# Delta rule: one key product a chunk, write keys through memory, exponents moved, output copies first

## The reference

```python
rk = rk / jnp.maximum(jnp.linalg.norm(rk, axis=-1, keepdims=True), 1e-12)      # read keys
wk = jnp.pad(rk[:, :, :-1], ((0, 0), (0, 0), (1, 0), (0, 0)))                   # write keys: one token later
L_mask = jnp.tril(jnp.exp(jnp.tril(cum[..., :, None] - cum[..., None, :])))     # decays inside a chunk
M = jnp.tril(-(wk_scaled @ jnp.swapaxes(wk, -1, -2)) * L_mask, -1)
A = solve_triangular(eye - M, eye, lower=True, unit_diagonal=True)
intra = jnp.tril(rk @ jnp.swapaxes(wk, -1, -2) * L_mask, -1)
# step over chunks, carrying the state S (128 x 128 for each batch and head)
v_new = A_i @ vsc_i - A_i @ wkd_i @ S
o_i = rkd_i @ S + intra_i @ v_new
S = ced_i * S + wkp_i @ v_new
```

## Time and profile before

| what | value |
|---|---|
| median of 3 runs | 2408.51 us (2408.32 to 2412.16) |
| time of the profiled execution | 2399.99 us |
| its span, first to last instruction | 2398.3 us |
| mean granted PE clock over the span | 0.965 |
| PE busy over the span | 2197.5 us (92%) |
| DVE, ACT, POOL busy | 1843.5, 1646.8, 1449.4 us |
| the first stage | 0 to 404.2 us, PE busy 336.67 us of it |

### The profile page before, as it was taken

The page is one execution under the profiler, slowest core; times in us unless marked ns, Lnnn a source line. Parts: engine busy times, 40 slices in busy tenths (PEclk is TensorE's granted clock), DMA queues, the critical chain, the costliest instruction groups (busy, mean ns, idle before and its releaser), DMA issues.

```text
span 2398.3 us, 36952 instructions
## 1 busy us (share of the span) xinstructions
PE 2197.5 (92%) x12464; PEld 1788.7 (75%) x12464; DVE 1843.5 (77%) x2832; ACT 1646.8 (69%) x2715; POOL 1449.4 (60%) x1026
## 2 busy tenths in 40 slices
PE   6799897999999999996999999999999999999986
PEld 4788796998898898884667667676676765776765
DVE  5574453667766666677989989989899899898995
ACT  6775542555555556666887788787877877888774
POOL 0236563111111113336988989889889898898895
PEclk8899998999999999997999999999999999999988
DMA  8434544566666654444655655555555555565563
GB/s 291 85 56 111 112 125 136 181 236 232 234 230 230 233 209 152 133 126 154 219 169 190 198 184 186 194 186 202 176 186 195 199 187 177 185 211 177 178 208 101
DMA packets 235434, 430.22 MB, mean 179 GB/s; under 512 B 35089, under 2 KB 117457, under 8 KB 235234
## 3 DMA queue, kind: packets, MB, share of 16 engines
q1 hardware_dynamic: 229090, 410.87, 53.0%
q0 software_dynamic: 6144, 16.79, 2.2%
HBM read 353.61 MB, written 73.96 MB: 178 GB/s over the span
## 4 chain that ended last, share of the span: by engine, by line
PE 54%; DVE 13%; issue 9%; ACT 9%; DMA 6%; POOL 6%; SPq 1%; another core or an unknown queue 1%; POOLq 1%; DVEq 0%; ACTq 0%
PE pb L1641 11%; PE pb L1614 11%; DVE pb L2094 6%; PE pb L2406 5%; PE pb L2411 5%; PE pb L994 3%; PE pb L2305 2%; PE pb L2432 2%; PE pb L2321 2%; DVE UU L2100 2%; DMA XB<-xnd 2%; PE pb L2330 2%; DMA CC<-bcd 2%; POOL UU L2019 2%; POOL UU L2027 1%
## 5 line engine op out<-in xcount | busy, mean ns | idle before, releaser
L2019 POOL TENSOR_TENSOR UU<-dx,BB 128x1024 f32<-128x1024 f32 x256 | 614.6, 2409 | 112.0 <-DMA BB<-bcd 83.6
L2231 ACT ACTIVATE pb<-dt,al 128x512 f32<-128x512 f32 x512 | 339.5, 685 | 149.4 <-DVE UU L2100 147.8
L2100 DVE TENSOR_TENSOR UU<-pb,CC 128x512 f32<-128x512 f32 x512 | 351.3, 686 | 24.3 <-DMA CC<-bcd 6.5
L2094 DVE TENSOR_TENSOR_SCAN pb<-pb,hs,UU 128x512 f32<-128x512 f32 x256 | 328.5, 1283 | 10.7 <-ACT pb L2231 7.4
L2094 DVE TENSOR_TENSOR_SCAN pb<-pb,UU 128x512 f32<-128x512 f32 x256 | 313.0, 1223 | 8.5 <-ACT pb L2231 7.9
L1381 POOL TENSOR_TENSOR clo_b<-craw_b,chi_b 128x1024 fp32r<-128x1024 f32 x22 | 62.3, 2830 | 405.9 <-ACT chi_b L1444 405.9
L1531 DVE TENSOR_TENSOR HL<-HF,HH 128x512 fp32r<-128x512 f32 x220 | 159.6, 728 | 179.9 <-ACT HH L1436 165.7
L2406 PE MATMUL pb<-HAh,WH 128*128 128x512 f32 x1024 | 282.7, 419 | 7.0 <-DVE dt L2075 5.1
L1431 ACT ACTIVATE HF<-pb,BU 128x512 f32<-128x512 f32 x192 | 132.3, 689 | 219.4 <-PE pb L1614 191.9
L2411 PE MATMUL pb<-HAl,WH 128*128 128x512 f32 x1024 | 259.7, 396 | 0.0
L1641 PE MATMUL pb<-W2h,HH 128*128 128x256 f32 x880 | 256.0, 291 | 1.0
(11 more groups left out here) (336 smaller groups left out, 4891.0 us busy)
## 6 DMA issues: line engine op xcount, KB each, us to landing
WH<-fhd SPq DMA_DIRECT2D x176, 512.0 KB, 3.5
BB<-bcd SPq DMA_DIRECT2D x256, 256.0 KB, 4.7
CC<-bcd SPq DMA_DIRECT2D x256, 256.0 KB, 5.0
raw<-in_w1a SPq DMA_DIRECT2D x23, 1024.0 KB, 7.3
raw<-in_w2a SPq DMA_DIRECT2D x23, 1024.0 KB, 7.4
craw_b<-in_fch SPq DMA_DIRECT2D x22, 512.0 KB, 5.9
fhd<-chi_b SPq DMA_DIRECT2D x22, 512.0 KB, 3.9
fld<-clo_b SPq DMA_DIRECT2D x22, 512.0 KB, 4.9
```

Of the source, the lines that this page charges most:

```text
L2019: e.tensor_tensor(ubuf(n)[:], dx[p][:], BB[n % 3][:].rearrange("p (a m) -> p a m", a=1).to_broadcast([P, 2, 512]), ALU.mult).then_inc(p_u. ...
L2094: e.tensor_tensor_scan(h_[:], h_[:], uu[:, c, :], first, ALU.mult, ALU.add).then_inc(v_sc.sem, 1)
L2100: e.tensor_tensor(uu[:, c, :], abank(n, c)[:], CC[n % 3][:], ALU.mult).then_inc(v_mu.sem, 1)
L2231: e.activation(abank(n, c)[:], dt[p][:, c, :], ACT.Exp, scale=al1[:, 2 * p + c, s:s + 1]).then_inc(c_a.sem, 1)
```

## The change

In every round the product `kk'` is gone, but for step 0. `kq'` moves from the end of the round to its head, and `mix` now reads it: M is written one column over and already transposed (tile MTB, two buffers), so that the transposes `MT'` and their copies go too. Its decays E are computed in the transposed sense, from a second row of sums (cumulated decay minus the logarithm of beta) which ZR now carries beside the first; ZR doubles to 128 x 4 x 256. `inner` moves to DVE's head of the round (iT gets two buffers).

The write keys' rows come no longer from transposes `wkT` and copies but through memory: SP writes the read keys of step n+2 to a tensor rkd (`keys_out`) and reads those of step n back one row earlier (`keys_in`).

On ACT the decays E and ET and the factor ez are computed a step further ahead, in the middle of the round, and the output copies OT stand in front, behind `vn`. POOL does `decayed` and `solve` before `upper`. SP starts `sums` at the head of its round.

```diff
-        order = ["kk'", "d4", "wkT", "wkS", "P4", "D4", "P5", "t5", "D5", "rkT''", "t6", "P6", "T6", "MT'", "vn", "v'", "o", "S", "kq'"]
+        order = ["kq'", "d4", "wkS", "P4", "D4", "P5", "t5", "D5", "rkT''", "t6", "P6", "T6", "vn", "v'", "o", "S"]
 ...
-                        ["d4", "wk", "rk''", "ETr'", "ET'", "t5", "ez'", "rc'", "rT''", "t6", "MT'", "vn", "Er''", "E''", "o"]) for h in range(2)]
-        g_pool = [Chunks(sem(f"g_pool{h}"), ["ETsel", "rkdT"], ["ETsel'", "rkdT'"]) for h in range(2)]
+                        ["d4", "rk''", "Er''", "E''", "t5", "rc'", "rT''", "ETr''", "t6", "ET''", "ez''", "vn", "o"]) for h in range(2)]
+        g_pool = [Chunks(sem(f"g_pool{h}"), ["ETsel", "rkdT", "ETsel'"], ["rkdT'", "ETsel''"]) for h in range(2)]
 ...
-                    e.dma_start(ZR[h][:], cumd.rearrange("(b n h) t -> n h b t", b=4, n=8)[n, h].rearrange("(o b) t -> o b t", o=1).to_broadcast([P, 4, P])).then_inc(s_zr, 16)
+                    e.dma_start(ZR[h][:].rearrange("p b k t -> p b (k t)"), cumd.rearrange("(b n h) t -> n h b t", b=4, n=8)[n, h].rearrange("(o b) t -> o b t", o=1).to_broadcast([P, 4, 2 * P])).then_inc(s_zr, 16)
 ...
+            def keys_out(n):
+                for h in range(2):
+                    e.wait_ge(*g_act[h].at("rk", n))
+                    e.dma_start(rkd[h, :, 1 + n * P:1 + (n + 1) * P, :].rearrange("b t d -> t b d"), TB[h]["rk"][:]).then_inc(s_rkd, 16)
+            def keys_in(n):
+                e.wait_ge(s_rkd, 32 + 32 * (n + 1))
+                for h in range(2):
+                    if n:
+                        e.wait_ge(*g_pe[h].at("S", n - 1))
+                    e.dma_start(TB[h]["wk"][:], rkd[h, :, n * P:(n + 1) * P, :].rearrange("b t d -> t b d")).then_inc(s_wk, 16)
 ...
             blocks(0)
+            sums(1)
             spread(0)
-            sums(1)
+            keys_in(0)
+            keys_out(1)
 ...
+                if n + 2 < NSEQ:
+                    sums(n + 2)
                 if n + 1 < NSEQ:
                     blocks(n + 1)
                 if n + 1 < NSEQ:
                     spread(n + 1)
+                if 0 < n < NSEQ - 1:
+                    keys_in(n)
                 if n + 2 < NSEQ:
-                    sums(n + 2)
+                    keys_out(n + 2)
 ...
-                    upper(n + 1)
                     decayed(n + 1)
                     solve(e, n + 1)
+                    if n + 2 < NSEQ:
+                        upper(n + 2)
 ...
-                e.tensor_tensor(M2[:, h], four(gbank("kk", n, h)), W["E"][:], ALU.mult).then_inc(g_dve[h].sem, 1)
+                e.wait_ge(*g_pe[h].at("kq", n))
+                e.wait_ge(*(g_pe[h].at("MT", 0) if n == 1 else g_pe[h].at("P6", n - 2)))
+                e.wait_ge(s_md, 128 * (n if n == 1 else n - 1))
+                e.tensor_tensor(MTB[n % 2][:, h, :, 1:P], four(gbank("kq", n, h))[:, :, 0:P - 1], W["E"][:, :, 1:P], ALU.mult).then_inc(g_dve[h].sem, 1)
 ...
                     for h in range(2):
                         mix(n + 1, h)
+                    for h in range(2):
+                        inner(n + 1, h)
 ...
-                    for h in range(2):
-                        inner(n + 1, h)
                     for h in range(2):
                         inverse(n + 1, h)
 ...
-                for h in range(2 if more else 0):
-                    turned("wkT", n, h, prev(n, h))
 ...
-                if more:
-                    for h in range(2):
-                        MT(n + 1, h)
 ...
                         e.wait_ge(*g_dve[h].at("vnt", n))
-                        e.wait_ge(*g_act[h].at("wk", n))
+                        e.wait_ge(s_wk, 16 + 32 * (n + 1))
                         product("S", n, h, W["wk"], W["vnt"])
-                if more:
-                    inner(n + 1)
```

More of the change, by code:

```diff
@@ L147, in program @@
         rows = [sbt(f"rows{i}", [P, 2, D]) for i in range(3)]
-        cumT = sbt("cumT", [64, P])
-        ZR = [sbt(f"ZR{h}", [P, 4, P]) for h in range(2)]
+        cumT = sbt("cumT", [64, 2, P])
+        ZR = [sbt(f"ZR{h}", [P, 4, 2, P]) for h in range(2)]
         a_end = at[0]
@@ L180, in program @@
         r_act = Count(sem("r_act"), ["exp", "p2"])
-        IDLE = {("wkS", 0), ("R", 0), ("S", NSEQ - 1), ("vnt", NSEQ - 1), ("wkT", NSEQ - 1), ("wk", NSEQ - 1)}
+        IDLE = {("wkS", 0), ("R", 0), ("S", NSEQ - 1), ("vnt", NSEQ - 1)}
         class Chunks:
@@ L316, in blocks @@
                 for q in range(8):
-                    e.dma_start(md[n, 16 * q:16 * q + 16], M2[16 * q:16 * q + 16, :, :, 16 * q:16 * q + 16]).then_inc(s_md, 16)
+                    e.dma_start(md[n, 16 * q:16 * q + 16], (MTB[n % 2] if n else MTB[1])[16 * q:16 * q + 16, :, :, 16 * q:16 * q + 16]).then_inc(s_md, 16)
             def spread(n):
@@ L452, in pool_a @@
             decayed(0)
+            upper(1)
             for n in range(NSEQ):
@@ L907, in decays @@
                             e.wait_ge(*g_pool[h].at("rkdT", n - 1))
-                        e.activation(TB[h]["ez"][:], ZR[h][:] if n else four(gbank("z", 0, h)), ACT.Exp).then_inc(g_act[h].sem, 1)
+                        e.activation(TB[h]["ez"][:], ZR[h][:, :, 0, :] if n else four(gbank("z", 0, h)), ACT.Exp).then_inc(g_act[h].sem, 1)
                     else:
@@ L934, in act_a @@
             rows_(1)
-            copy("MT", 0, "MT", "MT")
+            for h in range(2):
+                e.wait_ge(*g_pe[h].at("MT", 0))
+                e.activation(MTB[0][:, h], four(gbank("MT", 0, h)), ACT.Copy).then_inc(g_act[h].sem, 1)
             carried(0)
@@ L941, in act_a @@
             lower(1)
+            upper(1)
+            decays(1, "ET")
+            decays(1, "ez")
             for n in range(NSEQ):
@@ L944, in act_a @@
                 copy("d4", n, "d4", "Dm")
-                if more:
-                    copy("wk", n, "wkT", "wk")
                 if n + 2 < NSEQ:
                     rows_(n + 2)
-                if more:
-                    upper(n + 1)
-                    decays(n + 1, "ET")
+                    lower(n + 2)
                 if n == 1:
@@ L960, in act_a @@
                     turned_rows(n + 2)
+                    upper(n + 2)
                 copy("t6", n, "t6", "DT")
-                if more:
-                    copy("MT", n + 1, "MT", "MT")
+                if n + 2 < NSEQ:
+                    decays(n + 2, "ET")
+                    decays(n + 2, "ez")
                 copy("vn", n, "vn", "vn")
@@ L1023, in MT @@
                 e.wait_ge(*g_dve[h].at("M", n))
-                turned("MT", n, h, M2[:, h])
+                turned("MT", n, h, MTB[1][:, h])
             def y(n, b2):
@@ L1104, in pe_a @@
                 if more:
[L1105 to L1107 removed]
+                    inner(n + 1)
                 for h in range(2):
```

75 lines of the change are left out of this document (43 added, 32 removed).

## The result

The changed kernel takes 2422.58 us, median of 7 runs (2414.91 to 2430.87), the kernel before beside it 2408.51 us (2406.13 to 2412.16): ratio 1.0064, with a 95% interval of 1.0046 to 1.0083, so 14 us slower. Predicted were 2413 us (2390 to 2434), and 2404 to 2421 for the likeliest case alone: the time lies in the range, and 1.6 us above that case. The changed kernel's profiled execution has a span of 2421.9 us. Round n is PE's pass n, as in the prediction.

What follows compares the result with a forecast made beforehand. PE was taken to bound the first stage, busy 35.57 of 37.47 us in round 2. Terms -25.2 - 0.4 + 9.0 + 13.6 + 1.4 + 4.5 + 1.5 = +4.4 us on 2408.5 gave about 2413 us, range 2390 to 2434.

Steps and rivals of the forecast that it cites:

- the likeliest case: Whole kernel: about no change with a small loss, 2413 us, held from 2404 to 2421; chance 0.42.
- PE's time, -25.2 us: PE, rounds 0 to 6: a pair of products, wkT and MT go, 3.60 us a round, 25.2 us saved.
- T6, +9.0: PE before T6, rounds 0 to 5: waits for t6's copies behind ET's Relus, 1.5 us each, 9.0 us lost.
- D4, +13.6: PE before D4, rounds 0 to 6: waits for DVE's longer, later head of the round, 13.6 us lost together.
- y waits for the copies, +1.4: PE before y: waits for the second output copy, 0.2 us a round, 1.4 us lost.
- E, -0.4: ACT, round 0: E no longer stands in front of OT, 0.4 us gained.
- The end, +1.5: Round 7: the chain M, md, MB, solve, DT is no longer covered by the round's length, 1.5 us lost.
- The start, +4.5 (0 to 12.6): Before round 0: ZR queued ahead of MB delays it 5.5 us, less 1 us gained: 4.5 us lost.
- (1) PE's time comes through: Rounds: DVE and ACT hide more of the waits than forecast; 2388 to 2400 us, middle 2395; chance 0.27.
- (2) ZR late for E: ACT's E, first third of the round: waits 3.2 us for ZR in 5 rounds, 16 us more, 2429 us; chance 0.16.
- (3) The scatters: POOL's scatters clump behind `upper` and stall engines as in round 5: 11 us more, 2424 us; chance 0.10.
- (4) The keys through memory: Key copies collide with MB, so S waits 2 us in 6 rounds: 12 us more, 2425 us; chance 0.05.

Runs made afterwards that it cites:

- the ninth run: The changed kernel itself, unedited, measured again in another group of runs: 2370.2 us, ratio 1.0045 to the kernel before.
- the twelfth: The kernel before with one edit, step 1's spread sums issued ahead of step 0's blocks MB: 2364.42 us, ratio 1.0032.
- the eleventh run: The changed kernel with ET and ez behind vn's copies, iT between levels 5 and 6, ZR before md, round 2's routing later: 2347.02 us, ratio 0.9955.
- the sixth run: The changed kernel with one edit, ZR of step 1 issued before md of step 0: 2366.51 us, ratio 1.0023.

## Why the prediction was right, and where it was not

Direction and place were right: a small loss, 14 us where 4.4 were named, since PE's work does go and three waits take its place. The pair of traces without standstills (the ninth run and the twelfth, the kernel before with its sums first) prices the terms. There d4 starts at 98.70 us, 11.1 us later than before, and from d4 to the stage's end the changed kernel takes 275.25 us (373.95 less 98.70), the kernel before with its sums first 278.17 (372.60 less 94.43). So the rounds give 2.9 us, where the terms of the prediction other than the start come to -0.1.

- *PE's time, -25.2 us.* Borne out. From start to start in round 3 the three groups take 1.79, 0.87 and 0.94 us in the twelfth run and are gone in the ninth: 3.60 us. PE's busy time falls by less, from 35.05 to 32.02 us, since T6's products, which overlapped with those before them, now run by themselves behind their wait. With the next two terms, rounds without a standstill take 34.02 and 34.26 us; 34 to 35 were said.
- *T6, +9.0.* Measured 1.35 us in rounds 0 to 5, 8.1 us. But this is its idle part alone. **The step that failed inside the rounds is this one's silence on what PE does after it has stood**: the clock falls and the next products take up to twice as long. From T6's start to the start of the products for `o` it is 6.61 us where the clock stays (round 0 of the first trace) and 8.07 to 9.69 in rounds 1 to 5: 10.8 us in all, T6 itself included. In the ninth run it is 4.7 us, in rounds 0, 2 and 5; filling the gap was worth 7 us. The hint stood in the earlier trace rows: 0.89 and 0.92 in the rounds with the longest waits. I read it as a part of the standstill and gave no other wait such a price.
- *D4, +13.6.* In the ninth run its idle time is 0.5, 2.0, 5.4, 0.6, 0.8 and 1.3 us in rounds 0 to 5 and none in 6; less the 1.9 us of the kernel before in round 2 that is 8.7. In rounds 3 to 6 I had 1.5 each and 0.7 is the mean: DVE's list was added up too full, by its own overlap. In round 2 the routing counts in full, as said; moving it is worth 7 us of that round.
- *y waits for the copies, +1.4, and E, -0.4.* There is no idle time before y in any undisturbed round but the last, where it is 1.66 us in both kernels. So the first is nothing, and the 0.4 us of round 0 are gone as said.
- *The end, +1.5.* d4 of round 7 waits 0.4 us for DT, and from `y` of round 6 to `y` of round 7 it is 0.8 us longer than before (26.59 against 25.77). Its reason comes out in the faster kernels, where it decides every round.
- *The start, +4.5 (0 to 12.6).* **Measured 11.1: the term that was mis-sized most.** 6.9 come from the order alone, 2.0 from the width, 2.2 from POOL's work beside `solve`. I took one ZR of 0.23 MB and its 6.5 us for what lies in MB's way; there are two transfers, and SP's own issues of MB stood still behind them, 10.6 us for 3.6. That POOL had been idle there before, and that `upper(1)` and rkdT would now fall on DVE's steps, I had in no term. The 1 us that I had counted in return can't be seen: PE's 3.60 us, T6's wait and the 0.4 us before y alone would make round 0 some 2.6 us shorter, and in the first trace it is 2.4 (32.44 against 34.86).

Inside the rounds the measured terms -25.2 + 8.1 + 8.7 + 4.7 + 0.8 come to -2.9, as the two traces do; that they meet to the tenth is chance, since smaller terms are left out (the kernel before waits 1.4 us for its output copies in round 4). The sum -0.1 + 4.5 against -2.9 + 11.1 is the whole story without standstills (8.2 us in the traces, 10.6 by the ratio, the interval being 3.9 us either way). With them, the rounds of the first trace lose 8.85 instead of giving 2.9; what part of that is the standstills' and what the clock's no run separates. That the time came out in the range owes something to luck: D4, T6, y and the end were priced too high by 8 us together, the start too low by 6.6, and the clock was in no term.

The rivals. (1) PE's time comes through in the eleventh run alone, where four things are moved together, and even there in part. (2) ZR late for E did not happen in rounds 1 on: no row of ACT's E waits for it there, and at the start its time went by pieces, as taken. It did happen in front of round 0, 2.7 us. (3) The scatters: 9.4 to 10.4 us remain without them, so they are not the main cause; whether the change makes the standstills worse is open, and so is what causes these, since the group of runs made to settle it had none. (4) The keys through memory cost nothing: S starts with no wait in every undisturbed round. The rule that a tile of 128 partitions uses all 16 engines (the Trainium skill, "DMA: Bandwidth & Descriptors", section "Why a DMA increments its semaphore by 16 and not by 1") is not refuted by the 19.2% of the earlier trace rows. In the sixth run, with ZR alone in the queue, the engines' share is 38.6% from 59.2 to 60.8 us and 93.9% from 61.1 to 61.8, so 15 of 16 at work, and the rate is 87 and 73 GB/s: the share is no count of the engines that a transfer may use, and with more of them busy ZR moved no faster. Why the share is low elsewhere is open.

## What to carry to other kernels

Price a new wait on PE twice, as its idle time and as the products behind it at half clock; products that nobody needs, put into the gap, tell the two apart in one run. Taking one wait away moves the loss to the next in line while the same buffer or chain ties them (T6, iT and D4 here; MB and ZR at the start): alone, iT gained nothing, T6 3 to 5 us beside the changed kernel and ZR's earlier issue 5, and with the routing moved too they gain 21 to 23. And a transfer that is moved ahead of a short urgent one costs its own time in the queue, also when it is small.

## What was not expected of the hardware

- PE's granted clock fell to 0.52 of full behind 1.35 us of idle time, where PE had worked for 3 to 12 us since its last wait of half a us or more, and not each time: in five of six rounds in the first trace, in three of six in the ninth run. With the gap filled, in none.
- Two transfers of 512 pieces each to 128 partitions took 13.99 us at 512 B and 13.81 us at 1 KB a piece. What was queued behind them was read 1.96 us later with the wider pieces (87.03 against 85.07 us).
- Eight issues on SP's queue took 10.4 to 11.0 us instead of 3.6 with such transfers ahead of them: the queue holds up the issuing engine too.
- The kernel before took 2402.67 to 2408.51 us in two groups of runs and 2355.96 to 2359.74 in two others, 2% apart, with standstills of up to 10 us on PE, ACT and DVE together in the traces of the former and none in the latter. The three groups of experiments ran on three chips; whether it is the chip, no run tells.
